# A convolution with top-1 expert routing: copies of x, a slot's y, next weights and factors issued in another order

## The reference

```
y   = depthwise_causal_conv(x, taps, bias)             # [8, 512, 1024]
idx = argmax(y @ w_router, axis=-1)
out = x + einsum("h,fh->f", y[token], w_experts[idx[token]])   # for each token
```

## Time and profile before

| what | value |
|---|---|
| runs | 533.79, 535.79, 535.65 us; median 535.65 |
| profiled execution | 532.54 us, its span 530.7 us |
| granted TensorE clock, mean | 0.989 |
| TensorE matmul busy | 506.2 us (95%) |
| DVE, ACT, POOL busy | 286.1, 150.4, 132.9 us |
| DMA | 130.30 MB, mean 246 GB/s |

### The profile page before, as it was taken

How to read it: one execution, slowest core, us unless ns; L and a number is a source line. 1 busy time by engine, 2 the same in 40 slices (tenths; PEclk the granted TensorE clock), 3 DMA queues, 4 the chain that set the end, 5 groups by cost and what they waited for, 6 DMA issues and landing times.

```text
span 530.7 us, 9449 instructions
## 1 busy us (share of the span) xinstructions
PE 506.2 (95%) x2764; PEld 436.9 (82%) x2765; DVE 286.1 (54%) x383; ACT 150.4 (28%) x255; POOL 132.9 (25%) x148
## 2 busy tenths in 40 slices
PE   7998999997999996999999999999999999999995
PEld 6998989997788884888888888888888888888884
DVE  4956372677795025259794224482349224392860
ACT  2443434457001001047361001250026001250610
POOL 0003315060451112212331321221222222222322
PEclk9999999999899997999999999999999999999999
DMA  8976999997389997549999745588458845435445
GB/s 271 411 213 198 376 309 387 331 363 227 106 343 278 354 392 195 168 153 341 384 336 376 202 141 158 152 330 269 121 168 303 285 150 158 151 116 169 125 142 168
DMA packets 59621, 130.30 MB, mean 246 GB/s; under 512 B 12752, under 2 KB 32720, under 8 KB 59600
## 3 DMA queue, kind: packets, MB, share of 16 engines
q1 hardware_dynamic: 41984, 70.32, 42.5%
q0 software_dynamic: 14832, 54.27, 28.7%
q10 hardware_dynamic: 2784, 5.46, 3.3%
HBM read 94.56 MB, written 35.45 MB: 245 GB/s over the span
## 4 chain that ended last, share of the span: by engine, by line
PE 81%; DMA 5%; SPq 5%; issue 4%; DVE 3%; POOL 2%; ACT 0%; POOLq 0%; DVEq 0%
PE ps L833 61%; PE ps L788 20%; DMA ids_all<-y_sorted 3%; SPq L381 2%; SPq L283 1%; POOL y_sorted L889 1%; DMA factors<-factors_t 1%; DMA y_sorted<-rows,pos_i 1%; DVE x_row L681 0%; SPq L314 0%; DVE xs L499 0%; SPq L285 0%; ACT ys L434 0%; POOL x_row L894 0%; POOL out L901 0%
## 5 line engine op out<-in xcount | busy, mean ns | idle before, releaser
L833 PE MATMUL ps<-w_sb,ys 128*128 128x512 f32 x1680 | 385.8, 392 | 9.5 <-issue 9.5
L833 PEld LDWEIGHTS ps<-w_sb,ys 128*128 128x128 f32 x1680 | 318.1, 190 | 76.6 <-issue 10.1
L668 DVE STREAM_TRANSPOSE y_cols<-y_blk 128x1024 f32<-128x1024 f32 x36 | 44.8, 1244 | 169.8 <-PE ps L833 139.1
L788 PE MATMUL ps<-mats,xs 128*128 128x128 f32 x1024 | 117.3, 276 | 8.1 <-DVE xs L499 4.2
L788 PEld LDWEIGHTS ps<-mats,xs 128*128 128x128 f32 x1024 | 115.4, 192 | 9.6 <-DVE xs L499 4.8
L434 ACT CAST ys<-y_cols 128x1024 fp32r<-128x1024 f32 x36 | 37.9, 1053 | 281.8 <-DVE y_cols L668 267.7
L901 POOL DMA_INDIRECT out<-x_row,idx x35 | 43.2, 1236 | 92.0 <-DVE x_row L681 89.0
L659 DVE TENSOR_TENSOR w_sb<-w_raw,w_sb 128x1024 fp32r<-128x1024 f32 x56 | 64.3, 1219 | 3.2 <-ACT w_sb L429 2.5
L908 POOL COPY idx<-ids_all 128x1 int32 (+1 forms) x36 | 15.4, 427 | 180.7 <-DMA out<-x_row,idx 103.5
L429 ACT CAST w_sb<-w_raw 128x1024 fp32r<-128x1024 f32 x56 | 56.4, 1051 | 9.5 <-PE ps L833 8.0
L889 POOL DMA_INDIRECT y_sorted<-rows,pos_i x32 | 34.2, 1070 | 79.1 <-PE ps L788 59.7
(11 more groups left out here) (101 smaller groups left out, 41.4 us busy)
## 6 DMA issues: line engine op xcount, KB each, us to landing
w_raw<-experts SPq DMA_DIRECT2D x56, 512.0 KB, 8.2
y_blk<-y_sorted SPq DMA_DIRECT2D x152, 128.0 KB
xs<-x_both SPq DMA_DIRECT2D x15, 512.0 KB, 11.0
xs<-x_t SPq DMA_DIRECT2D x28, 256.0 KB, 5.8
xs<-x_t ACTq DMA_DIRECT2D x20, 256.0 KB, 7.2
w_first<-experts SPq DMA_DIRECT2D x8, 512.0 KB, 9.6
ids_all<-y_sorted SPq DMA_DIRECT2D x38, 1.0 KB
x_row<-x_rows,idx POOLq DMA_INDIRECT x36
```

Source lines behind the costliest of these rows:

```text
L668: V.transpose(y_cols[k][:, :, :].rearrange("p m (t i) -> p t m i", t=4), y_blk[:, k, :, :, :]).then_inc(y_blocks, 1)
L788: mm = nc.tensor.matmul(to, xs[:, n % X_RING, s % PACK, :], mats[:, s, :].rearrange("p (u n) -> p u n", n=SIDE), start=(s == sets[0]), sto ...
L833: mm = nc.tensor.matmul(out_ps[k][:, f * HALF:(f + 1) * HALF], ys[k][:, a, c, :], w_sb[:, c, b, f * HALF:(f + 1) * HALF], start=(c == 0 an ...
```

## The change

Five things are changed.
- Factors of pack 1 and of packs 2 and 3 are loaded through ACT's queue in place of SP's.
- In quarters 1 to 3 DVE makes the copies of packs n+4 and n+5 ahead of `place_rows`, and that of n+6 ahead of the lead's search.
- Slot 0's `y_blk` has a buffer of its own, and its y is loaded at pack 54, where a weight chunk was; the last two chunks go out at packs 58 and 62. It is turned ahead of the last two copies, and its split comes earlier on ACT and DVE. Slot 1's y waits for five split chunks in place of two; its turning comes behind `sum_most` and `low(0, 6)`. The other small buffers change places.
- `part` is one buffer in place of two, so ACT waits for both reductions of the quarter before from quarter 1 on.
- The y of slots 5 and 6 are loaded ahead of `w_raw[1]`. The first round of SP's loop is written out for this.

More of the change, by code:

```diff
@@ L50 @@
 MOST_BANKS = BANKS - 4
+Y_BANK = BANKS - 3
 def bank_sets(n):
@@ L282, in load_y @@
             for q in range(4):
-                queue.dma_start(y_blk[32 * q:32 * q + 32, k, :, :, :].rearrange("p t m f -> p t (m f)"),
+                queue.dma_start(y_blk[k][32 * q:32 * q + 32, :, :, :].rearrange("p t m f -> p t (m f)"),
                                 pieces[:, q]).then_inc(y_got[k], 16)
@@ L298, in load_x, with load_factors @@
                 queue.dma_start(xs[side:side + SIDE, s, :, :].rearrange("p c t -> p (c t)"), x_t[n - DOUBLED]).then_inc(x_in[s], 16)
+        def load_factors(queue, k):
+            a, b = FACTOR_PACKS[k]
+            cols = slice(0 if k == 0 else CH + a * PACK * (PHASES + EXPERTS), CH + b * PACK * (PHASES + EXPERTS))
+            queue.dma_start(factors[:, cols], factors_t[:, cols]).then_inc(factors_in[k], 16)
         @block.sync
         def _(sp):
[L302 to L305, removed]
             def lead_row(n):
@@ L311, in chunk, with load_lead_slot @@
                 return experts[bass.ds(e, 1), :, c, :].rearrange("e p f -> (e p) f")
+            def load_lead_slot(t):
+                sp.wait_ge(lead_known, t + 1)
+                row = lead_row(t)
+                sp.wait_ge(y_out[t % 2], (t // 2 + 1) * TPG * 16)
+                load_y(sp, row, t % RING, ids_all[:, t:t + 1, :])
             def load_slot(t, k):
@@ L328, in replace_raw @@
                                 sp.dma_start(w_raw[k][:, c, :], chunk(e, c)).then_inc(raw_in[k][c], 16)
-            load_factors(0)
+            load_factors(sp, 0)
             x_0 = xs[:, 0, :, :].rearrange("p c t -> p (c t)")
@@ L376, in _, with load_raw @@
             loads = sp.value_load(one_i[0:1, 1:2], min_val=0, max_val=EXPERTS - 1)
-            for k in range(2):
+            def load_raw(k):
                 with sp.If(k < loads):
@@ L419, in evict @@
                 to = rows[g % 2][:, :, sets[0] * CH:(sets[0] + m) * CH].rearrange("p j (c i) -> p j c i", i=CH)
-                nc.scalar.copy(part[:, g % 2, :, b], conv_bank(n)[:, PER_BANK * SIDE:]).then_inc(part_out, 1)
+                nc.scalar.copy(part[:, :, b], conv_bank(n)[:, PER_BANK * SIDE:]).then_inc(part_out, 1)
                 nc.scalar.copy(to, conv_bank(n)[:, 0:m * SIDE].rearrange("p (c j i) -> p j c i", j=PHASES, i=CH)).then_inc(conv_out, 1)
@@ L513, in sum_most @@
                 dve.wait_ge(part_out, g * BANKS + MOST_BANKS)
-                V.tensor_reduce(most[:, :], part[:, g % 2, :, 0:MOST_BANKS], AX.X, ALU.add).then_inc(most_sum, 1)
+                V.tensor_reduce(most[:, :], part[:, :, 0:MOST_BANKS], AX.X, ALU.add).then_inc(most_sum, 1)
             def choose(g):
@@ L525, in choose @@
                 flat = logits[:, :, :].rearrange("p t e -> p (t e)")
-                V.tensor_reduce(flat, part[:, g % 2, :, MOST_BANKS:], AX.X, ALU.add).then_inc(logit_sum, 1)
+                V.tensor_reduce(flat, part[:, :, MOST_BANKS:], AX.X, ALU.add).then_inc(logit_sum, 1)
                 dve.wait_ge(logit_sum, g + 1)
@@ L667, in turn_blocks @@
                     dve.wait_ge(gemm_chunk, (t - 1) * HC)
-                V.transpose(y_cols[k][:, :, :].rearrange("p m (t i) -> p t m i", t=4), y_blk[:, k, :, :, :]).then_inc(y_blocks, 1)
+                V.transpose(y_cols[k][:, :, :].rearrange("p m (t i) -> p t m i", t=4), y_blk[k][:, :, :, :]).then_inc(y_blocks, 1)
             def low_y(t, k):
```

19 lines of the change are left out of this document (3 added, 16 removed).

## The result

The changed kernel took 521.40 us (median of 6 runs, 518.95 to 524.16), and the kernel before 535.16 us beside it on the same chip (6 runs, 533.79 to 535.79): a ratio of 0.9753, with a 95% interval of 0.9718 to 0.9788. The profiled execution was the quickest of the six, 518.95 us with a span of 517.1; the profiled execution before had 532.54 and 530.7. Line 803 is now the convolution's matmul, 848 the product, 512 the copy of x, 672 a first chunk's `low`, 681 the turning and 686 `low_y`.

The account below looks back on a forecast made before the run. TensorE bounds the kernel, busy 506.2 of 530.7 us, leaving its idle and lower-clock time to win. Start 1.6, copies 4.2, slots 0 and 6 7.8 sum to 13.6 us: profiled 518.9, median 522.0, range 517.5 to 528.3.

Parts of the forecast that it names:

- the signs named in the prediction: Pack 2 near 9.0; no copy pauses; first product within 1 us; 1 to 2 us before slots 3, 5; full clock.
- Start, 1.6 us: First packs: with factors on ACT's queue, pack 2 starts at 9.0 in place of 10.62; 1.6 us won, bounds 0 and 2.57.
- ACT's queue does nothing for the start: Rival: moving the factors to ACT's queue wins nothing at the first packs, 523.6 us; chance 0.08.
- Copies, 4.2 us: Quarters 1 to 3: copies ahead of the placing remove all TensorE waits for copies of x, 4.2 us; bounds 0 and 4.2.
- The DMA rival, 0.14: Rival: DMA engines become the bound in the quarters; at worst start and quarters give all back, 527.9 us; chance 0.14.
- Slot 0: Convolution's end: first product at 129.8 for 133.87, last rank 1.5 us late; 4.1 us won, 1.73 of it clock.
- What eats this: Slots 3 and 5: their y comes only 0.4 us earlier, product 3 waits 1.2; of 4.1 us only 1.1 are left.
- Slot 5's 1.8 us: Ahead of product 5: due at 187.4, it starts at 189.2, since its y comes only 0.4 us earlier.
- Slot 6, 7.8 us with slot 0: Slot 6's y, issued directly behind slot 5's, lets product 6 start at 200.2, before 208.0 with clock; 7.8 us including slot 0.
- Slot 6's wait moves to a residual's x or slot 7's y, 0.10: Rival: the wait ahead of product 6 moves on; at most 5.03 and 1.7 us return, 528.8 us; chance 0.10.
- Slot 5's y is faster, 0.18: Rival: without the second weights beside it, product 5 starts at 187.4; 1.8 us more, 520.2 us; chance 0.18.
- Slower by slot 1's y, 0.04: Rival: slot 1's y lands up to 12.3 us late, delaying the rank and slots 3 and 5; 536.0 us; chance 0.04.

Follow-up runs that it names:

- the four parts alone: Four kernels, each the kernel before with one part: factors through ACT 1.0000, copies' order 0.9925, y of slots 5 and 6 ahead 0.9866, slot 0's y early 0.9977.
- the repeat: The changed kernel once more with no edit, on another chip, giving a second profile: 522.86 us, ratio 0.9782.
- the start alone: Kernel before with only the factors of packs 1 to 3 moved to ACT's queue: 535.41 us, ratio 1.0000.
- slot 0 alone: Changed kernel with the factors' queue, the copies' order and the order of slots 5 and 6's y as before: 534.64 us, ratio 0.9977.
- the copies alone: Kernel before with only the order of DVE's copies of x against the placing and lead search changed: 531.13 us, ratio 0.9925.

## Why the prediction was right, and which of its terms were not

The forecast for the profiled execution was 518.9 us and it took 518.95; 522.0 for the median, against 521.40. That the profile hit to 0.05 us is luck: it is the quickest of six runs, and in it two errors cancel, since the convolution gave 7.3 us for a forecast of 5.8 and the products 6.3 for 7.8. In the second profile of the same kernel (523.65 us) they gave 4.7 and 4.2. By the medians the whole was worth 13.2 and 11.7 us on the two chips, for a forecast of 13.6. Of the signs named in the prediction, pack 2 began near 9.3 (forecast 9.0), the copies' pauses and those ahead of slots 6 and 7 were gone; but the pause ahead of slot 3 was 3.76 us and not 1 to 2, and the lower clock was back in the products behind it.

- **Start, 1.6 us.** At the first rank it is about right: five kernels with the old start reached it at 41.9 us in the mean (41.05 to 43.12), nine with the new one at 40.6 (40.02 to 41.52). A cost that I had not listed is in this: with the factors on two queues the first pack itself began at 5.1 us in the mean, and with the old start at 4.2. At the end nothing of it can be measured (ratio 1.0000 alone; 0.9739 without it against 0.9753 and 0.9782 with it). The step that failed is that I carried this gain through: x of the last quarter came no earlier. The rival "ACT's queue does nothing for the start" has the right worth, nothing at the end, for another reason. In the kernel before, x of pack 1 goes out one issue late and x of pack 2 two, 0.95 us. The Trainium skill (DMA: Bandwidth & Descriptors, "Issuing engines are not separate DMA queues") says that issuing from several engines saves only the sequencer's time for the issues. The 1.2 us measured at the first rank, the difference of these means, lies between this and my 1.6, and the spread of the marks does not decide between them.
- **Copies, 4.2 us.** Right: 4.0 measured alone. The rows of before held no loss of clock behind these pauses, but two of the three other traces with the old order do (2.02 us of pause, then 28.69 us for the 240 matmuls that took 27.07), so the order can be worth 1.6 us more than its pauses. The second and third quarter also kept what they won (2.3 and 1.4 us by the ranks). What I had not listed is a pause of 1.02 us put down to "issue" in the last quarter of the kernel before, which stands in none of the rows. It was absent in the changed kernel's first profile and back in its second (1.04). It explains most of the convolution's 1.5 us beyond the forecast.
- **The DMA rival, 0.14.** Half true. Beyond the pauses for copies, TensorE stood for 1 us or more in all in the last quarter in 7 of the 11 profiles with the old queues, and the DMA engines are at 0.99 to 1.05 of their time from 108 to 120 there. But in the three kernels with two loads moved from ACT's queue to SP's it never stood, with the engines as full (1.00 to 1.04 from 104 to 116): so what bound was rather that a load waits behind ACT's wait, though that wait was also shorter in these three. It grew, from 4.25 us in the trace of before to 6.72 and 7.46 in the changed kernel's two; the prediction named this wait (4.50 us in quarter 2) and cost the waits there at nothing.
- **Slot 0.** First product within 1 us, rank 1.5 us late: 0.37 and 1.46. Won at this place are the 4.51 us pause and the clock, less 0.37 and 1.46: from the convolution's end to the products behind the rank it takes 6.45 us for 10.43, so 4.0 for a forecast of 4.1.
- **What eats this.** The mechanism is as forecast, the size not. POOL's last scatters began 7.6 us earlier than before where the convolution ended 7.3 earlier: 0.4 won, as forecast. I took slot 3's landing of 2.58 us from the one trace of before. Over eight profiles with this order of issues (before, the four parts alone, the changed kernel twice, and without its start) it was 2.58 to 5.63 us, and the one I sized from was the quickest. The pause ahead of slot 3 was 3.76 us, and the clock took 1.4 more (the 231 products behind it 54.25 us, at the rate of the 126 before 52.9), for a forecast of 1.2: the term that was mis-sized, by some 4 us in this profile, of which 2.2 are the landing, 1.4 the clock and 0.5 a later issue of y. Slot 5's 1.8 us did not appear in that profile, since slot 3's longer pause covered it, so that the products as a whole fell short by only 1.5; in later profiles with y of slot 5 behind the weights it was 2.2 to 4.5 us. In the repeat it was the other way round: 1.49 us ahead of slot 3, near the forecast, and 3.39 ahead of slot 5. So the two pauses are one term, forecast at 3.0 us and measured at 3.8 and 4.9, with the clock on top, which the forecast did not have.
- **Slot 6, 7.8 us with slot 0.** The reordering alone gave 7.2 us for the 5.03 and 1.7 us of the trace. The 1.7 is low: it takes the rate of 270 products as the full one. At that of 1344 later ones with no lower clock (304.94 us, in the kernel with slot 5's y moved) the 1392 lost 2.7 us. No pause is left ahead of slot 6 in any kernel that has it.
- **Slot 6's wait moves to a residual's x or slot 7's y, 0.10.** Not in the changed kernel. It came about, as both, in later kernels: slot 7's y once slot 5's had been moved, the residual's x once slot 7's had.
- **Slot 5's y is faster, 0.18.** Not so: over all traces slot 5's y took 11.9 to 15.4 us with slot 6's y behind it and 10.6 to 14.1 with the second weights there.
- **Slower by slot 1's y, 0.04.** Not seen: DVE waited 0.37 us for it in the changed kernel's first profile, and 0.62 at most in the others.

What stays open is why slot 5's y takes 10.6 us in one profile and 15.4 in another behind the same 4 MB, and why slot 3's is late when the gather follows it closely. Spreading the scatters over a longer stretch was not tried.

## What to carry to other kernels

A gain upstream is worth what is left of it at the next place where a transfer, not the engine, sets the time; so read the margin at each such place over several profiles, for a landing in one trace can be well below the usual (here 2.58 us, with a mean of 4.0 over eight). Where a small load stands in a queue behind megabytes, or behind a wait of the engine that issues it, change its place in the order before counting bytes. And when one late load is moved forward, look at its next-later sibling: here the wait went from slot 6 to 3 and 5, then to slot 7, then to its residual.

## What the runs showed of the hardware

A load in a queue behind large ones is late by far more than its size. Slot 3's y with its token numbers took 2.3 to 5.6 us with no weights ahead of it in its queue, and slot 5's 10.6 to 15.4 us behind 4 MB. An estimate: at the 364 GB/s of the window from 161.12 above, the 4 MB alone take 11.5 us.

TensorE's clock answered pauses unevenly. Ahead of the products, the 3.76 us pause was followed by a stretch at half of full speed (1.2 of 2.4 GHz; the window above has 0.56 in the mean), and so were the pauses of 3.15 to 6.3 us ahead of products in the other traces: at 1.4 to 2.8 us each, over the rate of the products around them. Among shorter ones the outcome differed: none behind 2.20 and 2.44 us, one behind 2.57 and 2.62 us, and two pauses of the same 3.10 us went both ways (without the start no lower clock, with slot 5's y moved a stretch of 3.4 us). In the convolution too: behind the pause of 2.02 us at pack 20 the clock stayed in the trace of before and in that of the start alone, and fell to half for 3.4 us with slots 5 and 6's y ahead and with slot 0 alone. With the start alone and the copies alone it also fell behind several short breaks close together, none over 1.05 us.

```profile
45.34 28.69 PE L794 MATMUL ps<-mats,xs 128*128 128x128 f32 x240 [2.02 <-DVE xs L505]
```

This line is of the kernel with slots 5 and 6's y ahead; the earlier trace rows has 27.07 us for the same work.

POOL's indirect DMA instruction was slower beside DVE's subtractions of two full tiles. In the changed kernel (timeline of both engines):

```profile
138.69 1.23 DVE L686 TENSOR_TENSOR ys<-y_cols,ys 128x1024 fp32r<-128x1024 f32 x1
138.75 2.01 POOL L904 DMA_INDIRECT y_sorted<-rows,pos_i  x1 [0.30 <-issue]
139.84 1.22 DVE L694 TENSOR_TENSOR x_row<-ps,x_row 128x1024 f32<-128x1024 f32 x1
```

It took 2.01 us here. From 60 us on in all traces, scatters with DVE idle or nearly idle beside them took 0.96 or 0.97 us, and the twelve that ran beside both of these subtractions 1.23 to 2.02; others were slowed too, as beside copies of x (up to 1.5). The last eight scatters took 11.8 us from the first's start to the last's end, 10.5 before, and slot 3's y was issued 0.5 us later than forecast.
